# A vision tower with routed experts on one core: copies of turned tiles, tables, experts' low parts and the output matrix's load moved

## The reference

```python
    h = jnp.concatenate([jnp.broadcast_to(cls_tok, (h.shape[0], 1, h.shape[2])), h], axis=1)
    h = h + _L0_attn_ref(_layernorm(h, axis=-1), ...)
    h = h + _L0_ffn_ref(_layernorm(h, axis=-1), ...)
...
        router_logits = jnp.einsum('bsh,he->bse', x, router_w) + router_b
        router_probs = jax.nn.softmax(router_logits, axis=-1)
        top_k_probs, top_k_indices = jax.lax.top_k(router_probs, K)
        top_k_probs = top_k_probs / jnp.sum(top_k_probs, axis=-1, keepdims=True)
        onehot = jax.nn.one_hot(top_k_indices, num_experts, dtype=x.dtype)
        gates = jnp.einsum('bsk,bske->bse', top_k_probs, onehot)
        expert_out = jax.nn.gelu(jnp.einsum('bsh,ehd->ebsd', x, expert_w) + expert_b[:, None, None, :])
        combined = jnp.einsum('bse,ebsd->bsd', gates, expert_out)
        return jnp.einsum('bsd,df->bsf', combined, out_w) + out_b
```

## Time and profile before

| | |
|---|---|
| three runs | 779.11, 781.23 and 782.02 us; median 781.23 |
| the profiled execution | 779.62 us |
| its span | 777.8 us |
| busy share of TensorE, VectorE, ScalarE, GpSimd | 87%, 68%, 52%, 19% |
| TensorE's share of the chain that ended last | 68% |
| granted clock of TensorE, mean | 0.954 |

### The profile page before, as it was taken

How to read it: one execution, slowest core, us unless ns; L and a number is a source line. 1 busy time by engine, 2 the same in 40 slices (tenths; PEclk the granted TensorE clock), 3 DMA queues, 4 the chain that set the end, 5 groups by cost and what they waited for, 6 DMA issues and landing times.

```text
span 777.8 us, 16638 instructions
## 1 busy us (share of the span) xinstructions
PE 679.1 (87%) x5653; PEld 545.2 (70%) x5654; DVE 532.4 (68%) x1219; ACT 405.3 (52%) x1058; POOL 148.6 (19%) x305
## 2 busy tenths in 40 slices
PE   3758888779999999999999999878468999998898
PEld 3457877767777686776868777645356888886686
DVE  4989895466778677777867776678873444446575
ACT  3835554476767676666766757572613333332111
POOL 5000000010121111102112110112032222226460
PEclk9879999989999999999999999999559999999999
DMA  7400345400000010000100004036326556557794
GB/s 223 159 0 1 137 101 146 96 2 1 3 24 31 0 54 0 27 27 13 40 0 33 21 27 174 31 106 242 155 69 202 162 163 164 163 167 230 250 320 151
DMA packets 54504, 76.11 MB, mean 98 GB/s; under 512 B 24617, under 2 KB 26921, under 8 KB 54338
## 3 DMA queue, kind: packets, MB, share of 16 engines
q1 hardware_dynamic: 41346, 42.56, 16.7%
q0 software_dynamic: 5920, 19.40, 9.6%
q10 hardware_dynamic: 7200, 13.63, 4.6%
HBM read 45.42 MB, written 30.16 MB: 97 GB/s over the span
## 4 chain that ended last, share of the span: by engine, by line
PE 68%; DVE 20%; issue 4%; DMA 3%; ACT 3%; POOL 1%; SPq 0%; ACTq 0%; DVEq 0%; POOLq 0%
PE ps L1943 42%; PE ps L2046 7%; PE ps L2056 4%; PE ps L2039 4%; PE ps L2096 3%; DVE ring L1376 3%; DVE ring L1377 3%; PE ps L1890 2%; DVE negmax L1447 2%; DVE ew_lo L1690 2%; PE ps L2063 1%; DMA b_in<-in_L_tok_B_ri_dram 1%; PE ps L2315 1%; PE ps L2088 1%; PE ps L1934 1%
## 5 line engine op out<-in xcount | busy, mean ns | idle before, releaser
L1013 ACT ACTIVATE pts<-ps 128x512 f32<-128x512 f32 x128 | 77.1, 602 | 108.3 <-PE ps L2046 108.3
L1005 ACT ACTIVATE prb<-ps,negmax 128x257 f32<-128x257 f32 x256 | 117.7, 478 | 4.7 <-DVE negmax L1447 3.7
L1447 DVE TENSOR_REDUCE negmax<-ps 128x2 f32<-128x514 f32 x128 | 82.5, 686 | 31.9 <-PE ps L2039 31.9
L2046 PE MATMUL ps<-ident,prb 128*128 128x128 f32 x512 | 83.9, 287 | 6.2 <-ACT pts L1013 3.0
L2046 PEld LDWEIGHTS ps<-ident,prb 128*128 128x128 f32 x512 | 57.2, 143 | 30.5 <-issue 11.7
L1456 DVE TENSOR_SCALAR prb<-prb,rrec 128x258 f32<-128x258 f32 x256 | 73.5, 352 | 2.3
L1177 ACT ACTIVATE rows<-ps 128x512 f32<-128x512 f32 x40 | 23.9, 598 | 88.0 <-DVE ps L1803 88.0
L1943 PE MATMUL ps<-ew_hi,xnT_hi 128*128 x160 | 67.4, 421 | 1.7 <-DVE xnT_lo L1723 1.7
L1943 PE MATMUL ps<-ew_lo,xnT_hi 128*128 x160 | 64.2, 401 | 0.0
L1943 PE MATMUL ps<-ew_hi,xnT_lo 128*128 x160 | 63.8, 399 | 0.0
L833 POOL DMA_INDIRECT rows<-xn_dram,token_of x40 | 40.5, 1014 | 108.9 <-PE ps L2096 89.6
(11 more groups left out here) (392 smaller groups left out, 1754.6 us busy)
## 6 DMA issues: line engine op xcount, KB each, us to landing
y_slots<-rows ACTq DMA_DIRECT2D x40, 256.0 KB
ew<-in_L_ffn_expert_w_dram SPq DMA_DIRECT2D x8, 1024.0 KB, 8.6
h_dram<-h_ob SPq DMA_DIRECT2D x17, 256.0 KB, 2.0
xn_dram<-tok SPq DMA_DIRECT2D x17, 256.0 KB, 2.2
h_late<-h_dram SPq DMA_DIRECT2D x15, 256.0 KB
out_dram<-h_late SPq DMA_DIRECT2D x14, 256.0 KB
y_slots<-u_sb SPq DMA_DIRECT2D x9, 256.0 KB, 6.5
tok_dram<-so SPq DMA_DIRECT2D x4, 512.0 KB, 3.2
```

What stands on the lines that cost most here:

```text
L1005: e = act.activation(prb[:, u % 2, j, 0:KEYS], ps[:, j, 0:KEYS], ACT.Exp, bias=negmax[:, u % 2, j:j + 1], accum_out=rowsum[:, u % 2, j:j + 1])
L1013: act.activation(pts[:, slot:slot + 2, :, st * P:(st + 1) * P], ps[:, 4, :].rearrange("p (h t s) -> p h t s", h=2, t=HALVES), ACT.Copy).th ...
L1447: dve.tensor_reduce(negmax[:, u % 2, 2 * b:2 * b + 2], ps[:, 2 * b:2 * b + 2, 0:KEYS], AX_X, ALU.max, negate=True).then_inc(s["dve_max"], 1)
L2046: mm = pe.transpose(ps[:, 4, (2 * j + tt) * P:(2 * j + tt + 1) * P], prb[:, u % 2, 2 * b + j, tt * P:(tt + 1) * P], ident[:, :])
```

## The change

Four things are moved; no work is added or left out, except that one DMA becomes four.

1. `KEPT_BY_DVE` names only tiles of the first two groups: the two copies that VectorE made in the fourth group are ScalarE's. ScalarE makes the high part of expert 3 between the third group's copies and its logits, and only expert 4's behind the last logits.
2. `picked`, `inside` and `cum` get a place that does not overlap the normed tiles. GpSimd fills `inside` without waiting; the wait for the stored tiles stands ahead of `of_tile` on ScalarE and on VectorE. SyncE issues the last stores first and the loads of experts 6 and 7 behind them. TensorE's two products of row counts change places, with a signal for each.
3. VectorE makes the low parts of experts 4 and 5 ahead of the first slot tile, and those of 6 and 7 behind the second tile's (before: 4, 5 and 6 ahead, 7 behind).
4. The output matrix is loaded in four pieces, each after one more turn of a slot tile but one, and the two early token tiles behind them in the same manner. Its high and low parts are made at the end of the slot stage.

```diff
-    KEPT_BY_DVE = [n < 4 * EARLY_QUADS and n % 2 == 0 or 4 * EARLY_QUADS + 4 <= n and n % 2 == 1 for n in range(NT)]
+    KEPT_BY_DVE = [n < 4 * EARLY_QUADS and n % 2 == 0 for n in range(NT)]
...
             keep_h(NB - 1, 0)
-            sp.wait_ge(s["pe_cls_projected"], 1)
-            for e in range(6, NE):
-                load_expert(e)
             keep_h(NB - 1, 1)
...
             sp.dma_start(xn_dram[CLS * P:, :], tok[:, CLS, :]).then_inc(s["stored_xn"], 16)
+            sp.wait_ge(s["pe_cls_projected"], 1)
+            for e in range(6, NE):
+                load_expert(e)
...
-            sp.wait_ge(s["pe_slot_turned"], 3)
-            sp.dma_start(ow[:, :, :], out_w.rearrange("(k p) d -> p k d", p=P)).then_inc(s["loaded_out_w"], 16)
+            for k in range(KC):
+                sp.wait_ge(s["pe_slot_turned"], 4 + 2 * k)
+                sp.dma_start(ow[:, k, :], out_w[k * P:(k + 1) * P, :]).then_inc(s["loaded_out_w"], 16)
             for t in range(EARLY_H):
+                sp.wait_ge(s["pe_slot_turned"], 4 + 2 * (KC + t))
                 sp.dma_start(of_end(t), h_dram[t]).then_inc(s["loaded_h"], 16)
...
             pool.memset(tiles_to[:, :, 0:4], 0.0).then_inc(s["pool_sums_cleared"], 1)
-            pool.wait_ge(s["pe_xn_turned"], NT)
-            pool.wait_ge(s["stored_xn"], 16 * NT)
             pool.memset(inside[:, :, :], 1.0).then_inc(s["pool_sums_cleared"], 1)
...
             for q in range(EARLY_QUADS, len(QUADS)):
-                for j in range(len(QUADS[q])):
-                    if not KEPT_BY_DVE[n]:
-                        keep_xnT(n)
-                    n += 1
+                for n in range(4 * q, 4 * q + len(QUADS[q])):
+                    keep_xnT(n)
+                if q == EARLY_QUADS:
+                    hi_expert(3)
                 keep_lgT(q)
 
-            for e in range(3, 5):
-                hi_expert(e)
+            hi_expert(4)
...
             act.wait_ge(s["dve_hit"], 1)
+            act.wait_ge(s["stored_xn"], 16 * NT)
             act.activation(of_tile[:, :, 1, :], hit[:, :, :], ACT.Copy, scale=part[:, 0:1]).then_inc(s["act_places"], 1)
...
             gelu(1, 1, True)
-            act.wait_ge(s["loaded_out_w"], 16)
-            act.activation(ow_hi[:, :, :], ow[:, :, :], ACT.Copy).then_inc(s["act_out_w_high"], 1)
...
             store_slots(SLOTS - 3, 1)
+            act.wait_ge(s["loaded_out_w"], 16 * KC)
+            act.activation(ow_hi[:, :, :], ow[:, :, :], ACT.Copy).then_inc(s["act_out_w_high"], 1)
             gelu(SLOTS - 2, 0, False)
...
             for q in range(EARLY_QUADS + 1, len(QUADS)):
-                for n in range(4 * q, 4 * q + len(QUADS[q])):
-                    if KEPT_BY_DVE[n]:
-                        keep_xnT(n)
                 take_logits(q - 1)
...
+            dve.wait_ge(s["pe_ranks"], 2)
             then(dve.scalar_tensor_tensor(out=first_slot[:, :], in0=tiles_to[:, 1, 3:3 + NE], scalar=float(P),
...
             dve.wait_ge(s["dve_hit"], 1)
+            dve.wait_ge(s["stored_xn"], 16 * NT)
...
-            for e in range(LOWS_IN_ATTENTION + 1, NE - 1):
+            for e in range(LOWS_IN_ATTENTION + 1, LOWS_IN_ATTENTION + 3):
                 lo_expert(e)
...
-            lo_expert(NE - 1)
+            for e in range(LOWS_IN_ATTENTION + 3, NE):
+                lo_expert(e)
...
             lo_xs(SLOTS - 1, 1)
+            add_bias(SLOTS - 2, 0)
             dve.wait_ge(s["act_out_w_high"], 1)
             dve.tensor_tensor(ow_lo[:, :, :], ow[:, :, :], ow_hi[:, :, :].bitcast(F32), ALU.subtract
                               ).then_inc(s["dve_out_w_low"], 1)
-            add_bias(SLOTS - 2, 0)
             add_bias(SLOTS - 1, 1)
...
-            pe.matmul(ps[:, 0, 0:NE], before[:, :], row_count, start=True, stop=True)
             pe.matmul(ps[:, 1, 0:NE], all_one[:, :], row_count, start=True, stop=True).then_inc(s["pe_ranks"], 1)
+            pe.matmul(ps[:, 0, 0:NE], before[:, :], row_count, start=True, stop=True).then_inc(s["pe_ranks"], 1)
```

More of the change, by code:

```diff
@@ L107, in vit_tower_kernel @@
             of_tile = sb(in_routing, "of_tile", [P, COLS, 2, SLOTS], F32R)
-            picked = sb(in_routing, "picked", [P, NE, COLS])
-            inside = sb(in_routing, "inside", [P, NE, COLS])
-            cum = sb(in_routing, "cum", [P, NE, COLS])
         with ExitStack() as to_end:
@@ L303, in vit_tower_kernel @@
         stores_used = sb(ffn, "stores_used", [P, 1], mybir.dt.int32)
+        with ExitStack() as in_routing:
+            picked = sb(in_routing, "picked", [P, NE, COLS])
+            inside = sb(in_routing, "inside", [P, NE, COLS])
+            cum = sb(in_routing, "cum", [P, NE, COLS])
         h_early = sb(ffn, "h_early", [P, EARLY_H, D])
@@ L416, in vit_tower_kernel @@
             "pe_logits": "a tile's logits",
-            "pe_ranks": "entries in earlier rows, and in all rows",
+            "pe_ranks": "entries in all rows, then in earlier rows",
             "pe_token_of": "tile and place of every slot's token",
@@ L1148, in hi_turned @@
                                ).then_inc(s[done], 1)
-            n = 4 * EARLY_QUADS
             for q in range(EARLY_QUADS, len(QUADS)):
-                for j in range(len(QUADS[q])):
-                    if not KEPT_BY_DVE[n]:
-                        keep_xnT(n)
-                    n += 1
+                for n in range(4 * q, 4 * q + len(QUADS[q])):
+                    keep_xnT(n)
+                if q == EARLY_QUADS:
+                    hi_expert(3)
                 keep_lgT(q)
-            for e in range(3, 5):
-                hi_expert(e)
+            hi_expert(4)
             act.wait_ge(s["dve_gate_gap"], 1)
@@ L1505, in keep_xnT @@
             def keep_xnT(n):
+                q, j = n // 4, n % 4
                 dve.wait_ge(s["pe_xn_turned"], n + 1)
-                q, j = n // 4, n % 4
-                if q < EARLY_QUADS:
-                    dst, bank = xnT_early[:, q], 7
-                else:
-                    dst, bank = xnT[:, q % 2], n % 4
-                dve.tensor_copy(dst[:, :, j * P:(j + 1) * P], ps[:, bank, :].rearrange("p (k t) -> p k t", k=KC)
+                dve.tensor_copy(xnT_early[:, q, :, j * P:(j + 1) * P], ps[:, 7, :].rearrange("p (k t) -> p k t", k=KC)
                                 ).then_inc(s["dve_xnT_kept"], 1)
```

## The result

The changed kernel takes 771.42 us (median of four runs, 769.77 to 771.83); the kernel before, timed beside it, 781.61 us (779.11 to 782.02). The ratio is 0.9865, with a 95% interval of 0.984 to 0.989. The forecast was 772.3 us. The profiled execution took 771.67 us against 779.62 before, 7.95 us less; the medians are 10.2 us apart. Four executions (two of the kernel before, at 970 and 974 us, one of e2 at 2744, one of e3 at 1098) show a mean granted clock of 0.24 to 0.65 and are left out of the medians here.

A forecast was written before the change was run, and what follows sets the result against it. TensorE was taken to bound the kernel, time being won only where it waits or runs at its lower clock. Gains of 3.05 + 0.9 + 4.65 = 8.6 us gave 772.6 from the 781.23 median; forecast 772.3, range 769.8 to 776.5.

The forecast's parts named there:

- The sum: Total gain at the start of tile 4's product in the slot stage: 3.05 + 0.9 + 4.65 = 8.6 us.
- A: Router: ScalarE copies the fourth group, so its logits start 1.7 us earlier and, at full clock, take 0.9 less.
- the row counts' swap: Routing: of TensorE's two pairs of products, the one VectorE needs first goes first; 0.45 us, bounds 0 and 0.59.
- the clock falls in the router as before: Rival, chance 0.12: TensorE still pauses in the norms, its clock falls, 0.9 us of gain goes; 773.5 us.
- B: Routing: sums' tables in their own place, last stores ahead of experts 6 and 7; waits hidden, cost 0, gain 0.
- C: Start of the slot stage: one of three low parts leaves the way of the first tile; 0.9 us, bounds 0 and 0.9.
- VectorE has no slack left: Slot tile 2: VectorE lets it start at 579.8, TensorE is there at 579.9; cost 0, up to 0.5 us.
- D: Slot tiles 0 to 4: output matrix in pieces, its parts at the end, removes the stall; 4.65 us, 3.0 if clock falls.
- the rival on them: Rival, chance 0.06: the output matrix's and token tiles' six transfers hold up gathers, costing 3 to 6 us; 775.5 to 778.5.
- Gathers late beside low parts: Rival, chance 0.06: tile 3's gather issue waits for VectorE's two low parts, 1.2 us lost; 773.8 us.

The follow-up runs named there:

- e2: Changed kernel with the output matrix as before: one transfer, its high and low parts made early; 776.92 us, ratio 0.9957.
- e3: Changed kernel with the output matrix loaded whole at the third turn, both token tiles right behind it, its parts still made at the end; 776.68 us, ratio 0.9934.
- e1: Changed kernel with the fourth group's two copies back on VectorE; 775.32 us, ratio 0.9901.
- e5: Changed kernel with low parts as before: experts 4, 5 and 6 ahead of the first slot tile, 7 behind the second; 772.0 us, ratio 0.9879.
- e11: The changed kernel itself, unedited, timed again on another chip; 767.65 us, ratio 0.9896.
- e4: Changed kernel with the sums' tables over the normed tiles again and experts 6 and 7 loaded ahead of the last stores; 775.29 us, ratio 0.993.
- e12: Changed kernel with only the sums' tables over the normed tiles again, the new order of stores and loads kept; 770.84 us, ratio 0.9883.
- e6: Changed kernel with 9, 30 and 28 extra unread products keeping TensorE busy in routing; 772.1 us, ratio 0.988.
- e10: Changed kernel with VectorE's five last low parts made later, plus 5, 30 and 13 unread products on TensorE in routing; other chip, 763.84 us, ratio 0.9842.
- e7: Changed kernel with the low parts of experts 3, 4 and 5 made by GpSimd during routing; 778.77 us, ratio 0.9973.
- e9: Changed kernel with VectorE's five last low parts made later, each product waiting for its own expert only; other chip, 767.43 us, ratio 0.9886.

## Why the prediction was right, by its steps

**The sum** of 8.6 us met 8.54 at tile 4's product, or 8.72 from the last norms: 3.31 up to the table `hit` (predicted 3.05), 0.80 from there to the first product (0.9) and 4.61 from the first product to tile 4's (4.65). The predicted marks were fourth group's logits at 540.8, first product at 571.3, tile 2's at 579.9 and tile 4's at 586.3; the rows have 540.77, 571.34, 579.97 and 586.38 (the last three as the chain shows them). The clock is 1.00 from the second tile on.

**A**, 1.7 + 0.9, measured: 1.88 for the start of the logits (2.44 us behind the last norms, before 4.32) and 0.86 for their length; the row counts' swap, predicted at 0.45, gave 0.43 (3.31 at `hit` less 2.88 at the running sum). Both profiles kept the clock through the pause of the norms, and there the mechanism was as predicted. What the prediction had too small is the price if that fails. In e3 the copies are on ScalarE and the logits still start at 3.85, in e1 they are on VectorE and start at 4.32: once the clock has fallen in the pause of the norms, the copies' place is worth 0.47 us at the logits, and the running sum starts at 11.77 and 11.47, later than the 11.28 of before. So the rival "the clock falls in the router as before", given 0.12 and priced at 0.9 us, costs 3.4 when it comes true. It did so in one of the eleven profiles, after's and ten experiments', that have the copies on ScalarE and nothing added in the pause; two of the eleven, e5 and e11, had a pause of only 0.43 and 0.44 us. Of all profiles with a pause of 1.74 to 1.78, eleven with before's and e1's, it fell in two, e1 and e3. That it fell in neither of the two that the sum compares is luck. What decides it stays open: in the changed kernel, e1 and e3 the pause is the same 1.74 to 1.77 us, and TensorE had been busy right before it in all three.

**B**, cost 0: right, and without it 2.75 us would have been taken back (e4), "nearly all of A", as predicted. The explanation was half right: the order of the stores does it alone (e12), and with it the tables' own place is not needed.

**C**, 0.9 at the first product: a little large. Before against after gives 0.80 there, e5 0.67, and nothing at tile 4, where an earlier clock made up for it. "VectorE has no slack left" was nearly right: tile 2's low part ends at 579.49, 0.24 us before TensorE begins the tile at 579.73, and where TensorE comes earlier (e6) it waits for VectorE.

**D**, 4.65: measured 4.61 between the two kernels; undone it costs 5.15 (e2). The prediction took the stretch as one and did not say which of the two edits brings it. Nearly half, 2.4, is the load's own effect on the gather beside it (e3), so the later split alone is not enough. The reverse, pieces with the split left early, was not run. The six small transfers held nothing up; the rival on them fell.

**Gathers late beside low parts** did not come about, because tile 3's gather was issued at 571.55, a microsecond ahead of the low parts at 572.55. The mechanism shows in two other rows. In e5 the gather issued at 569.34 takes 2.59 us; the three low parts beside it end at 564.42 + 6.69 = 571.11, and the issue ends at 571.93, 0.82 later, near a free one's 0.94. In the changed kernel the issue at 565.96 takes 1.77 in the same way, with the boundary of two low parts at 566.85. The rule of the Trainium skill that the prediction cited fits both. The same section also reports a probe in which a `tensor_tensor` did not stall a DMA; these two rows, in which such a subtraction seems to hold up a gather's issue, don't agree with that.

**From the span to the medians:** the sum gave 771.0 for the profiled execution and 772.6 for the median; the forecast says 772.3, and the prediction gives no reason for the 0.3 less. The profiled execution took 771.67, 0.5 of it in the combine stage, and the median lay 0.25 below it instead of 1.6 above. The two errors partly cancel: that 772.3 came within 0.9 us of 771.42 says less for the prediction than the marks in the trace do. The range's lower end has a slip as well: 781.23 - 8.6 - 2.1 is 770.5, not 770.

## What to carry to other kernels

Read a small wait on a shared engine together with the clock behind it: a copy that was 1.8 us late stood beside a fall worth half as much again, and whether the fall comes is not decided by that copy alone. Split a megabyte's load when it lies beside gathers, even if nobody waits for it, and put stores that free a buffer ahead of loads that are wanted late. Where two engines hold the same point, an edit to one of them can measure as nothing or as a loss: try both together before either is dismissed. And put the mark at which experiments are compared behind all that an edit moves: tile 4's bias showed e10 at 2.4 us, tile 8's at 1.6.

## What was not expected of the hardware

- TensorE's clock fell with TensorE fully busy: in e6 it is 1.00 in 557 to 558 us and 0.54 in the next, amid the 34 products with 80 columns, with busy 1.00 in both. In e10 the same products kept 1.00 throughout. Ahead of them TensorE idled 0.97 us in e6 and not at all in e10; whether this idle or the narrow products brought the fall is open.
- A VectorE comparison of 0.44 us took 4.7 beside a GpSimd subtraction (e7).
- One stage differed with the chip: the combine took 62.4 to 62.9 us in all three kernels on the chip of e9 to e11, and 65.9 to 68.6 elsewhere, and the kernel before was some 5.7 us faster there too. Why is not known. A time from one chip can't be set against a time from another.
